# Last MoE stage: experts picked from the sum ahead of the layer norm, rows scattered from X and gathered by token

## The reference, cut to what matters

```python
x = layernorm(x + power_attention(x))          # B=2, T=1024, C=128, 16 heads
x = layernorm(x + moe_by_expert(x))            # 16 experts, each takes its top 256 tokens
x = layernorm(x + latent_attention(x))         # softmax attention, 16 heads of 8, W_o at its end
# the stage that the change is about:
gates = softmax(x @ Wg)                        # 8 experts, x is 2048 x 128 after the third layer norm
top_g, top_i = top_k(gates, 2)
top_g = top_g / top_g.sum(-1)
y = einsum('etf,efd->etd', silu(x @ W1[e]) * (x @ W3[e]), W2[e])      # D=128, F=256
x = layernorm(x + sum over the two chosen e of top_g * y[e])
```

## Time and profile before

| | |
|---|---|
| median of three runs | 1048.37 us |
| the profiled execution | 1049.71 us |
| its span, first to last instruction | 1048.0 us |
| TensorE matmul busy | 881.6 us (84%) |
| VectorE busy | 708.7 us (68%) |
| ScalarE busy | 558.5 us (53%) |
| GpSimd busy | 437.1 us (42%) |
| granted clock, mean | 0.907 |

### The profile page before, as it was taken

How to read it: one execution, slowest core, us unless ns; L and a number is a source line. 1 busy time by engine, 2 the same in 40 slices (tenths; PEclk the granted TensorE clock), 3 DMA queues, 4 the chain that set the end, 5 groups by cost and what they waited for, 6 DMA issues and landing times.

```text
span 1048.0 us, 18020 instructions
## 1 busy us (share of the span) xinstructions
PE 881.6 (84%) x5997; PEld 437.4 (42%) x5997; DVE 708.7 (68%) x1480; ACT 558.5 (53%) x659; POOL 437.1 (42%) x829
## 2 busy tenths in 40 slices
PE   6699999999999877599947988999999988768771
PEld 4222233222223544389943533333333332258771
DVE  6779999999999767544426796778777844035145
ACT  3488898889889531222214304555555565444331
POOL 5154552453353600178871402333333333725761
PEclk9599999999999999799986578999999998889886
DMA  5961001101200402047744423211320110447873
GB/s 174 219 150 47 21 26 45 35 10 45 67 19 1 140 14 73 8 119 185 193 50 131 142 93 93 73 54 60 93 78 16 46 48 2 153 114 226 282 259 93
DMA packets 74751, 96.84 MB, mean 92 GB/s; under 512 B 9706, under 2 KB 55626, under 8 KB 71210
## 3 DMA queue, kind: packets, MB, share of 16 engines
q1 hardware_dynamic: 65696, 84.90, 27.3%
q0 software_dynamic: 8128, 9.59, 4.4%
q10 hardware_dynamic: 864, 1.57, 0.4%
HBM read 74.96 MB, written 24.22 MB: 95 GB/s over the span
## 4 chain that ended last, share of the span: by engine, by line
PE 47%; DVE 24%; issue 10%; POOL 9%; ACT 4%; DMA 4%; SPq 1%; DVEq 0%; ACTq 0%; POOLq 0%
PE acc_ps L873 10%; DVE mx L569 6%; PE acc_ps L1215 6%; PE tail_ps L1161 5%; DVE R L1748 4%; POOL moe_rows L2414 4%; PE causal_ps L1198 4%; POOL sent_rows L2488 3%; DVE tails L1754 3%; PE causal_ps L835 3%; PE causal_ps L1362 2%; PE causal_ps L846 2%; POOL G L2405 2%; ACT EX L1596 1%; PE tail_ps L835 1%
## 5 line engine op out<-in xcount | busy, mean ns | idle before, releaser
L1596 ACT ACTIVATE EX<-causal_ps 128x1024 f32<-128x1024 f32 (+1 forms) x160 | 147.0, 939 | 155.5 <-PE causal_ps L1198 154.5
L569 DVE TENSOR_REDUCE mx<-tail_ps 128x1 f32<-128x512 f32 x266 | 157.6, 634 | 39.7 <-PE tail_ps L1164 21.7
L1455 ACT ACTIVATE R<-R 128x2048 f32<-128x2048 f32 (+1 forms) x80 | 134.7, 1737 | 0.5 <-DVE R L1748 0.5
L2465 POOL TENSOR_TENSOR pacer<-eps_ln 128x1 f32<-128x1 f32 x160 | 32.1, 201 | 209.1 <-ACT EX L1596 208.3
L1198 PE MATMUL causal_ps<-QE,KE 75*128 75x512 bf16 (+3 forms) x384 | 103.6, 342 | 7.8 <-DVE mx L569 3.1
L1161 PE MATMUL tail_ps<-KM,QM 72*128 72x512 bf16 (+1 forms) x320 | 102.5, 347 | 8.8 <-DVE mx L569 3.0
L1748 DVE TENSOR_SCALAR R<-causal_ps 128x1024 f32<-128x1024 f32 (+1 forms) x88 | 94.0, 1070 | 15.3 <-PE causal_ps L835 14.2
L1462 ACT ACTIVATE R<-R 128x1792 f32<-128x1792 f32 (+4 forms) x80 | 100.5, 1268 | 0.0
L1754 DVE TENSOR_REDUCE tails<-causal_ps 128x1 f32<-128x768 f32 (+4 forms) x96 | 92.9, 968 | 10.6 <-PE causal_ps L846 9.8
L1215 PE MATMUL acc_ps<-EX,VS 128*32 128x512 f32 (+3 forms) x768 | 87.1, 529 | 3.0 <-POOL EX L2468 2.9
L2325 POOL TENSOR_TENSOR R<-R 128x512 f32<-128x512 f32 (+2 forms) x64 | 87.4, 1382 | 1.3
(11 more groups left out here) (332 smaller groups left out, 1680.1 us busy)
## 6 DMA issues: line engine op xcount, KB each, us to landing
ring<-e_pack SPq DMA_DIRECT2D x46, 384.0 KB, 4.0
QS<-q_parts SPq DMA_DIRECT2D x8, 576.0 KB
KS<-k_parts SPq DMA_DIRECT2D x24, 192.0 KB
QM<-q_parts SPq DMA_DIRECT2D x8, 576.0 KB
KM<-k_parts SPq DMA_DIRECT2D x24, 192.0 KB
QE<-q_parts SPq DMA_DIRECT2D x8, 576.0 KB
KE<-k_parts SPq DMA_DIRECT2D x24, 192.0 KB
wg<-in_wg_t SPq DMA_DIRECT2D x16, 256.0 KB, 3.0
```

Of the source, the lines that this page charges most:

```text
L569: return reduce(mx[:, par, hh, o0:o0 + step * (cnt - 1) + 1:step], scores[:, 0:cnt * w].rearrange("p (c w) -> p c w", w=w), AX.X, op, **how)
L1455: act.activation(R4[:, rp, h0:h0 + 2, 0:width], R1[:, rp, h0:h0 + 2, 0:width], ACT.Square).then_inc(squared, 1)
L1596: act.activation(EX[:, rp, hh, 0:width], causal_ps[hh % 2][:, 0:width], ACT.Exp, scale=float(D) ** -0.5).then_inc(exp_done, 1)
```

## The change

**Picking the experts.** The third layer norm subtracts a token's mean and divides by its deviation. The change takes the mean out of the gate instead: gate1 minus its column means (`centre_gate`, on a copy of the gate in every partition, gate_all, 512 KB in SBUF, loaded behind gate1) times the turned sum (X turned plus W_o times Y, made turned by `times_w_turned` with W_o as the standing operand) gives logits which only lack the division by the token's deviation. This does not change their order, so `gate_max` and `gate_picks` choose from them; `gate_scaled` brings in the deviation later, for the shares alone. `gate_picks` takes the greatest, blanks it and takes the greatest again, on 8 values per token, where the comparison before took 8x8. `turn_normed` is gone.

**Layer norms.** Batch 0's takes its reciprocal root on VectorE with three Newton steps (`scales_by_steps`); batch 1's sum is made in PSUM (`tokens` puts X there through the identity, `times_w(..., onto=True)` adds to it), and its moments and X come from there.

**Quad 7's masks** go from GpSimd to VectorE (`hide_later`, a minimum of 128x128 with `cap`, which holds 3e38 or 0). GpSimd's sends of batch 0 stand by themselves, from X, without the copies. Batch 1's whole routing goes ahead of batch 0's tiles.

**Results.** Each pair of tiles is stored in order (`store_pair`, SyncE's queue, y_rows), and 16 indirect DMAs per batch gather a token's two rows (`fetch`, GpSimd, into `back`). `load_back` and `give_back` are gone. Batch 1's last layer norm goes by parts of two tiles.

```diff
@@ SyncE's queue @@
+            sp.dma_start(gate_all[:, :], a["gate1"].rearrange("d e -> (d e)").unsqueeze(0).broadcast_to([P, P * E1])
+                         ).then_inc(f_gate_in, 16)
...
+            def store_pair(b, q):
+                t0, n = 2 * q, pair_tiles(q)
+                u = b * TILES + t0
+                sp.wait_ge(y_sb, u + n)
+                sp.dma_start(y_rows[b][t0 * P:(t0 + n) * P, :]..., y_f[:, u:u + n, :]).then_inc(y_out[b], 16)
...
+            for at in range(RING, B * PAIRS):
+                if at == PAIRS:
+                    load_tokens(1)
+                    sp.wait_ge(f_owner, 2)
+                load_pair(at // PAIRS, at % PAIRS)
+                store_pair((at - RING) // PAIRS, (at - RING) % PAIRS)
+            for q in range(PAIRS - RING, PAIRS):
+                store_pair(1, q)
@@ TensorE @@
+            def times_w_turned(n, bank, onto=False):
+                pe.wait_ge(yt_sb, CH + n + 1)
+                pe.matmul(banks[bank], w_o[:, :], YT[:, n % 2, :], start=not onto, stop=True, skip_group_check=onto
+                          ).then_inc(xt_full, 1)
...
             exp_quad(NQ - 2, NQ // 2 - 1, 0, False, beside=[
-                [], [(0, lambda: project_first(0, 0)), (0, lambda: project_first(1, 0)),
-                     (0, lambda: project_first(0, 1)), (0, lambda: project_first(1, 1))],
-                [], [(0, lambda: turn_normed(0)), (0, lambda: turn_normed(1))], [(0, lambda: route_half(0, 4))]])
+                [], [(0, lambda: turn_first(0)), (0, lambda: turn_first(1))],
+                [(0, lambda: times_w_turned(0, 4)), (0, lambda: times_w_turned(1, 5))],
+                [(0, lambda: times_first(0)), (0, lambda: times_first(1))], [(0, lambda: route_half(0, 4))]])
...
+            tokens_turned(2, 1)
+            tokens_turned(3, 3)
             run_all(exp_sums(NQ - 1, 1, NS - 1))
             pe.wait_ge(f_placed, 1)
             turn_exp(NQ - 1)
-            turn_y(1, 2, 4)
-            turn_y(1, 3, 5)
...
-            begin_tiles(0)
-            tile(0, 0)
-            turn_normed(2)
...
+            turn_y(1, 2, 0)
+            turn_y(1, 3, 2)
+            tokens(2, 6)
+            times_w_turned(2, 1, onto=True)
+            times_w_turned(3, 3, onto=True)
+            tokens(3, 7)
+            times_w(1, 2, 6, onto=True)
             route_half(1, 4)
+            times_w(1, 3, 7, onto=True)
             rank(1, 5)
+            for b in range(B):
+                begin_tiles(b)
+                for t in range(TILES):
+                    tile(b, t)
@@ VectorE @@
+            centre_gate()
+            for n in range(CH // B):
+                copy_turned(n, 4 + n)
+            for n in range(CH // B):
+                residual_turned(n)
...
+            hide_later(0, 0)
+            hide_later(0, 1)
             exp_normalise(NQ - 2)
+            hide_later(0, 2)
+            hide_later(0, 3)
+            for hh in range(3):
+                hide_later(1, hh)
+            gate_places(0, 5)
+            hide_later(1, 3)
+            gate_scaled(0)
+            gate_owners(0)
+            for s in range(2, NS):
+                for hh in range(HQ):
+                    hide_later(s, hh)
             exp_normalise(NQ - 1)
+            dve.wait_ge(out_full, CH + 3)
+            link(moments_of(range(KT, KT + CT), in_bank))
+            gate_max(1, 4)
+            gate_picks(1)
+            dve.wait_ge(out_full, CH + 4)
+            moments_of(range(KT + CT, NT), in_bank).then_inc(ln_var, 1)
+            gate_places(1, 5)
+            scales_of(0, KT, KT)
+            for n in range(CH // B, CH):
+                scaled(range(n * CT, (n + 1) * CT), in_bank)
             hidden(0, 0)
...
@@ GpSimd @@
-            hide_later(NQ - 1, 1, take=False, after=send_beside)
...
+            for b in range(B):
+                pool.wait_ge(f_placed, b + 1)
+                for i in range(KT):
+                    if i % CT == 0:
+                        pool.wait_ge(ln_x, 2 * CH + (b * KT + i) // CT + 1)
+                    send(b, i)
+            pool.wait_ge(y_out[0], 16 * PAIRS)
+            for i in range(KT):
+                fetch(0, i, scattered[i // CT])
+            pool.wait_ge(y_out[1], 16 * PAIRS)
+            for i in range(KT):
+                fetch(1, i, gathered[i // PART])
```

More of the change, by code:

```diff
@@ L171 @@
 FIRST_TURN = 8
-XT2_BANK = (4, 5, 4, 5)
 TILES = T * TOP // P + E1 - 1
-ROW = P + 1
 EW = 3 * F1
@@ L2224, in _ @@
-            gate_logits(0, 4)
-            exp_normalise(NQ - 2)
-            gate_probs(0)
-            gate_compare(0)
-            gate_ranks(0)
-            send(0)
-            gate_places(0, 4)
-            gate_owners(0)
-            gate_shares(0)
-            exp_normalise(NQ - 1)
-            for n in range(CH // B, CH):
-                residual(1, n, 2 + n)
-                moments(2, n)
-            hidden(0, 0)
-            hidden(0, 1)
-            standardise(2, 2)
-            hidden(0, 2)
@@ L2241, in _, with add_choices @@
-            standardise(2, 3)
-            hidden(0, 3)
-            send(1)
-            hidden(0, 4)
-            gate_logits(1, 4)
-            hidden(0, 5)
-            hidden(0, 6)
-            gate_probs(1)
-            gate_compare(1)
-            hidden(0, 7)
-            gate_ranks(1)
-            hidden(0, 8)
-            gate_places(1, 5)
-            hidden(0, 9)
-            gate_owners(1)
-            hidden(0, 10)
-            gate_shares(1)
-            for t in range(11, TILES):
+            def add_choices(tiles, arrived, count):
+                dve.wait_ge(arrived, count)
+                for c in range(TOP):
+                    for t in tiles:
+                        ins = dve.scalar_tensor_tensor(Z[:, t, :], back[:, c, t, :], share[:, t // KT, c, t % KT:t % KT + 1],
+                                                       (Z if c else X)[:, t, :], ALU.mult, ALU.add)
+                    link(ins)
@@ new lines, in sum_tiles @@
+            def sum_tiles(t0, n, arrived, count):
+                tiles = range(t0, t0 + n)
+                add_choices(tiles, arrived, count)
+                return moments_of(tiles, summed)
+            centre_gate()
[3 more added lines that the diff above has]
+                residual_turned(n)
+            for n in range(CH // B):
+                residual(1, n, 4 + n)
+                link(moments_of(range(n * CT, (n + 1) * CT), summed))
```

406 lines of the change are left out of this document (200 added, 206 removed).

## The result

The changed kernel takes 1041.37 us (median of 5 runs, 1039.38 to 1042.70), where the kernel before takes 1048.37: a ratio of 0.9931, 95% interval 0.9911 to 0.9952. It is faster, by 7 us, and not by the 18.4 that were forecast. The profiled execution took the median, 1041.37, with a span of 1039.5 us beside 1048.0 before.

What follows compares the result with a forecast made beforehand. TensorE's waits in quads, handover, gap and batch 1, plus the end without TensorE, were taken as the bound. Terms 0 -6.3 +3.2 -10.3 -6.2 -8.3 +9.5 = -18.4 from 1049.7 gave 1031.3, less 1.3: 1030; range 1019 to 1042.

Steps and rivals of the forecast that it cites:

- Quad 6: Stretch beside quad 6: TensorE's old 3.5 us stop traded for a 4 us one behind gate_all; 0, ends -5 and +2.
- Quad 7: Stretch beside quad 7: waits for sel and GpSimd's masks go, some work is added; -6.3 us, ends -9 and -1.
- Handover: From quad 7's last sum to the first `hidden`: no token wait but a longer chain, 20.7 instead of 17.5; +3.2 us.
- Tiles of batch 0: Batch 0's tiles no longer share engines with batch 1's routing: 35.5 instead of 45.8 us, -10.3.
- Gap: Between the batches: tokens and first weight pairs there or about to be; 3.5 instead of 9.7 us, -6.2.
- rival 1: Transfers set the tiles' pace, tokens and weights meeting at the gap; costs 6 us, 1036; chance 0.17.
- Tiles of batch 1: Batch 1's tiles: 34.4 instead of 42.7 us, with 1 us for the sums put between them; -8.3.
- End: After the last tile: 16 gathers in a row, then the last part; 31.2 instead of 21.7 us, +9.5, ends +7 and +18.
- The rule that was weighed: Quad 7: VectorE's minima could wait up to a send's length beside GpSimd's sends; the sum took nothing for it.
- rival 2: VectorE is late in the quads with masks or sel, so stops and slow stretches stay; +5 us, 1035; chance 0.13.
- rival 3: gate_all lands in time, so quad 6 has no stop; 1025 us; chance 0.16.
- rival 4: Slower gathers at the end: spacing 1.86 gives 1038, from 2.7 us the gain is gone; chances 0.05 (1.5 to 2.6), 0.04 (slower).

Runs made afterwards that it cites:

- experiment 2: The changed kernel with both gate loads issued before the store of quad 7's maxima, ahead of quad 7's key and query loads; 1035.22 us, ratio 0.9867.
- experiment 3: The changed kernel with the sum over gate_all reading elements side by side instead of every eighth; one execution, the sum took 1.22 us instead of 1.98.
- experiment 1: The changed kernel with VectorE's centring of the gate moved behind quad 6's copies of YT and residuals; 1035.05 us, ratio 0.9859.
- experiment 7: The changed kernel with quad 7's masks on GpSimd again and eight of batch 0's sends between them; 1047.06 us, ratio 0.9982.
- experiment 9: The changed kernel with the edits of experiment 1, experiment 2 and experiment 4, plus batch 1's tokens loaded in three pieces between weights; 1026.65 us, repeated 1028.88 us.
- experiment 4: The changed kernel with each of the two blocks of sums in batch 1's tiles split into three pieces; 1037.90 us, ratio 0.9888.
- the last version: The kernel of experiment 9 with results sent by tile, rows copied by GpSimd, and batch 0's result loads taken apart; 1024.93 us, ratio 0.9773.

## Why the prediction was wrong, and where it was right

The sign, the stages and most terms came out; the size did not. 1030 was forecast, 1041.37 came, inside the range by less than a microsecond.

- **Quad 6, the step that failed first.** "I take 854" for gate_all's landing, 1.1 us for its sum, "the old stop and the new are worth the same". It landed at 856.2, because 512 KB that take 3.8 us by themselves took 7.5 behind the key and query loads (experiment 2). The sum took 1.98 us: the estimate came from copies of neighbouring elements, and this one strides (experiment 3). VectorE went on at 858.4, and TensorE stopped for 6.8 us instead of 4. The greater error lies in "the same". Without the new wait quad 6 takes 30.9, which is 1.6 less than before, where the forecast had -5 for a load that is there in time; with it, 5.9 more, where it had 0, and +2 at the late end of the landing (856). What the old stop of 3.5 us had cost by itself no run shows, since the change also puts new products in the quad: TensorE is busy in it for 27.27 us before and 28.67 in experiment 1, at clocks of 0.89 and 0.91. What the runs do show is that both together give 1.6 back (1.3 to 3.4 in the seven profiles without the wait), and that the wait takes 7.5.
- **Quad 7: right in its sum, -6.2 for -6.3, and in part by luck.** No wait for sel, one for masks (1.5 us, with the slow stretch behind it, that had been put at 2.2). But the parts are not those of the forecast, which had 5.2 us for sel and 4.7 for the masks. With the masks on GpSimd again and no wait for sel the quad takes 34.7, 0.9 less than before (experiment 7), so the masks' engine is worth some 5.3 and the picks far less than 5.2. And the same quad took 27.9 to 30.6 us in other runs that leave it as it is, a change of -7.7 to -5.0.
- **Handover: right, +2.4 for +3.2.** The first tile's turn at 924.31 is 14.5 us behind the last sum (15.5), the first `hidden` 19.9 (20.7).
- **Tiles of batch 0: right, -11.5 for -10.3.**
- **Gap: half.** 6.0 us instead of 3.5. The tokens and the first pair were asked for in time, but 1.5 MB of tokens stood ahead of the weights that were needed first. "Tokens and the first pairs are there or about to be" failed on the second. With the tokens spread it is 2.5 (experiment 9). This is rival 1, and in the changed kernel only there: in the tiles weights were never late by more than 0.5 us in this profile.
- **Tiles of batch 1, the second step that failed.** 34.4 us were forecast, 40.5 came. "1 for the sums put between them" did not ask how long one piece is. A block of 3.7 us is longer than the 1.45 us of a tile and the one `hidden` that runs ahead; it stopped TensorE twice for 2 us, which costs 3.6 us at an equal clock. Cut to pieces of at most 1.3 us, the stage takes 34.3 (experiment 4). The other 2.6 us came with a clock of 0.92, for which the forecast had no term; how much of that the stops bring is open.
- **End: +7.3 for +9.5.** The first gather starts 1.9 us behind the last y and not 2.8, the fifteen spacings are 18.8 us and not 19.5, the last landing 2.56 and not 2.7, and the last part 5.7 and not 6.2.
- **The rule that was weighed** changed nothing. All 32 minima took 281 to 294 ns; the first send starts at 894.11 us, the last minimum at 905.9. The view of that one line of VectorE in the changed kernel (ns min/median/max):

```profile
L2228 DVE TENSOR_TENSOR EX<-EX,cap x32: 281/286/294, 882.6 to 905.9; 128x128 f32<-128x128 f32 x32
```

The 32 sends took 954 to 1136 ns, median 958, the first ten of them beside minima. None of the minima is longer beside a send, so in this kernel the Trainium skill's rule (SBUF — State Buffer, Who interferes with whom) had no price.

The other rivals: VectorE was late in the quads only by 1.5 us in quad 7 (rival 2), gate_all was not in time (rival 3), the gathers were as fast as those of the earlier trace rows (rival 4).

## What to carry to other kernels

When a step takes work away from one wait and puts another wait in its place, price each by itself, and from a row: here the new stop of 6.8 us cost 7.5, and taking the old one of 3.5 us away, with the new products in its place, gave back 1.6. Work that is put between the steps of a pipeline is priced by its longest piece against the slack of one step, and not by its total alone: here 3.6 us for two blocks of 3.7. And a load that nobody needs yet goes behind those that somebody waits for: the gate matrix ahead of the quad's loads, the tokens between the weights.

## What the runs showed of the hardware

- A load of 512 KB that hands the same 4 KB to all 128 partitions landed 3.5 to 3.9 us after its issue where it was issued first (six profiles), and 6.4 to 7.5 us behind 1.15 MB of other loads (seven).
- VectorE's sum of 1,024 elements to 8 took 1.98 to 2.02 us with 32 bytes between neighbours and 1.22 us side by side.
- The same quad 7 took 30.4 us at a granted clock of 0.81 and 27.9 at 1.00. So two profiles of kernels whose quads hold the same instructions differ by 4.3 us (61.3 and 57.0 for both quads), and a gain of that size is read from stages at like clocks and from the runs' median, not from one span.
- GpSimd issued the indirect DMAs of 128 rows that gather at a spacing of 1.25 us and those that send at 1.26; 46 of the latter in a row are 58 us, and in the last version GpSimd had no pause from batch 1's first row to its last result.
